# Putting DVE's remainders of one step between the block sums of the next one, in a three-product fp32 matmul

## The reference

```python
w = jnp.einsum('bpf,mf->bpm', features, W_ft) + b_ft      # features (1024, 2, 5128), W_ft (512, 5128), fp32
accumulator = stm * w                                     # stm (1024, 2, 1)
l1_x = jnp.clip(accumulator, 0.0, 1.0).reshape(features.shape[0], -1)
l2_x = jnp.clip(l1_x @ W1.T + b1, 0.0, 1.0)               # W1 (32, 1024)
return l2_x @ W2.T + b2                                   # W2 (1, 32)
```

## Time and profile before

| | us |
|---|---|
| median of 3 runs | 432.38 (429.82 to 434.44) |
| time of the profiled execution | 432.02 |
| its span, first to last instruction | 430.2 |
| PE busy | 407.0 (95%) |
| DVE busy | 349.6 (81%) |
| ACT busy | 196.2 (46%) |
| DMA queue q1, share of 16 engines | 66.9% |
| mean granted TensorE clock | 0.988 of full speed |

### The profile page before, as it was taken

The page is one execution under the profiler, slowest core; times in us unless marked ns, Lnnn a source line. Parts: engine busy times, 40 slices in busy tenths (PEclk is TensorE's granted clock), DMA queues, the critical chain, the costliest instruction groups (busy, mean ns, idle before and its releaser), DMA issues.

```text
span 430.2 us, 4578 instructions
## 1 busy us (share of the span) xinstructions
PE 407.0 (95%) x1756; PEld 323.3 (75%) x1756; DVE 349.6 (81%) x321; ACT 196.2 (46%) x176; POOL 13.2 (3%) x32
## 2 busy tenths in 40 slices
PE   6969999979999989998999999999999899999995
PEld 4747777858777868786878888878788778888862
DVE  3887888896899989979899877897887975698625
ACT  4464454343448444424444674363444448444300
POOL 2090000000000000000000000000000000000000
PEclk9999999989999999998999999999999999999999
DMA  7999797876867666663666766658667766778200
GB/s 237 387 239 269 219 267 247 253 226 200 264 227 244 223 233 235 244 226 143 244 245 244 240 222 237 240 205 337 239 235 238 240 194 195 240 231 254 96 2 0
DMA packets 27300, 96.37 MB, mean 224 GB/s; under 512 B 3432, under 2 KB 6384, under 8 KB 22032
## 3 DMA queue, kind: packets, MB, share of 16 engines
q1 hardware_dynamic: 26656, 95.44, 66.9%
q0 software_dynamic: 624, 0.66, 0.8%
HBM read 96.08 MB, written 0.00 MB: 223 GB/s over the span
## 4 chain that ended last, share of the span: by engine, by line
PE 65%; DMA 15%; DVE 12%; issue 5%; SPq 2%; ACT 1%; DVEq 0%
PE sums L496 63%; DMA xs<-x_p 15%; DVE x_lo L400 5%; DVE w_lo L397 1%; DVE xs L374 1%; PE sums L554 1%; PE sums L598 1%; DVE ws L378 1%; DVE x_lo L352 1%; DVE c_all L413 1%; ACT x_hi L275 0%; SPq L209 0%; DVE c_all L477 0%; DVE ws L364 0%; DVE xr L454 0%
## 5 line engine op out<-in xcount | busy, mean ns | idle before, releaser
L496 PE MATMUL sums<-x_lo,w_hi 128*128 128x512 f32 x560 | 178.0, 396 | 13.8 <-DVE x_lo L400 13.6
L496 PE MATMUL sums<-x_hi,w_hi 128*128 128x512 f32 x560 | 178.0, 396 | 3.2 <-ACT x_hi L264 2.3
L496 PE MATMUL sums<-x_hi,w_lo 128*128 128x512 f32 x560 | 177.2, 395 | 0.2 <-DVE w_lo L347 0.2
L289 ACT ACTIVATE x_hi<-xs 128x2048 fp32r<-128x2048 f32 x67 | 128.7, 1921 | 79.6 <-DVE xs L384 34.9
L400 DVE TENSOR_TENSOR x_lo<-xs,x_hi 128x2048 fp32r<-128x2048 f32 x67 | 153.0, 2284 | 0.0
L496 PEld LDWEIGHTS sums<-x_lo,w_hi 128*128 128x128 f32 x560 | 104.9, 190 | 42.2 <-issue 21.0
L496 PEld LDWEIGHTS sums<-x_hi,w_hi 128*128 128x128 f32 x560 | 106.4, 191 | 29.2 <-ACT x_hi L264 2.8
L496 PEld LDWEIGHTS sums<-x_hi,w_lo 128*128 128x128 f32 x560 | 106.8, 191 | 23.5 <-DVE w_lo L347 0.6
L284 ACT ACTIVATE w_hi<-ws 128x512 fp32r<-128x512 f32 x67 | 42.5, 634 | 116.9 <-PE sums L496 42.1
L397 DVE TENSOR_TENSOR w_lo<-ws,w_hi 128x512 fp32r<-128x512 f32 x67 | 45.9, 684 | 14.7 <-DMA ws<-w_p 14.7
L384 DVE TENSOR_TENSOR xs<-xs 128x2048 f32<-128x2048 f32 x20 | 45.8, 2288 | 8.0 <-DMA xs<-x_p 8.0
(11 more groups left out here) (59 smaller groups left out, 88.7 us busy)
## 6 DMA issues: line engine op xcount, KB each, us to landing
xs<-x_p SPq DMA_DIRECT2D x40, 1024.0 KB, 5.6
xs<-x_p SPq DMA_DIRECT2D x57, 512.0 KB, 5.6
ws<-w_p SPq DMA_DIRECT2D x43, 256.0 KB, 3.2
ws<-w_p SPq DMA_DIRECT2D x17, 384.0 KB, 3.4
ws<-w_p SPq DMA_DIRECT2D x20, 128.0 KB, 4.1
open_x<-x_p SPq DMA_DIRECT2D x2, 512.0 KB, 6.9
stm_all<-stm SPq DMA_DIRECT2D x1, 1024.0 KB, 7.5
open_x<-x_p SPq DMA_DIRECT2D x2, 256.0 KB, 3.8
```

Source lines behind the costliest of these rows:

```text
L289: nc.scalar.activation(x_hi[:, g % HI, :, :], x_pair(g), ACT.Copy).then_inc(x_hi_ready, 1)
L496: return nc.tensor.matmul(sums[:, bank, :], w[:, wslot, wpos, m * P:(m + 1) * P], x[:, xslot, xpos, c * BANK:(c + 1) * BANK], start=start, ...
```

## The change

`sums_of` is split into `w_sums_of` (w sum, in pass 0 also the kept one) and `x_sums_of`, and `low_step` into `w_low` and `x_low`. The loop now calls, for step g: w_low(g), w_sums_of(g+1), x_low(g), x_sums_of(g+1). The small subtraction of g = 8 goes ahead of x_low. In the opening `sums_of` is still one piece, but its kept w sum now stands ahead of its x sum. The instructions are the same ones, in the same number; SP's, ACT's and PE's programs are the same.

```diff
--- before.py
+++ after.py
@@ -353,49 +353,61 @@
                                             x_hi[:, g, pos, a:b].bitcast(F32), ALU.subtract)\
                         .then_inc(open_lo, 1)
 
-            def sums_of(g):
+            def w_sums_of(g):
                 f, k = pass_of(g)
-                i, j, n = raw_w(g, 0), raw_x(g, 0), g % RAW
-                opening = g < OPEN
+                i, n = raw_w(g, 0), g % RAW
                 dve.wait_ge(w_loaded[n], w_count(g))
                 if f == 0:
-                    if opening:
+                    if g < OPEN:
                         dve.wait_ge(open_w_loaded[g], 16)
                     nc.vector.tensor_tensor(ws[:, i + 1, :], ws[:, i + 1, :], ws[:, i + 2, :], ALU.add)\
                         .then_inc(w_sum, 1)
+                    dve.wait_ge(w_sum, g + 1)
+                    a11 = open_w[:, g, :] if g < OPEN else ws[:, i, :]
+                    nc.vector.tensor_tensor(ws[:, KEPT + k, :], ws[:, i + 1, :], a11, ALU.subtract)\
+                        .then_inc(s_kept, 1)
+                elif f == 1:
+                    nc.vector.tensor_tensor(ws[:, i, :], ws[:, i, :], ws[:, i + 1, :], ALU.subtract)\
+                        .then_inc(w_sum, 1)
+                elif f == 2:
+                    dve.wait_ge(s_kept, K_PAIRS)
+                    nc.vector.tensor_tensor(ws[:, i + 1, :], ws[:, i + 1, :], ws[:, KEPT + k, :], ALU.subtract)\
+                        .then_inc(w_sum, 1)
+
+            def x_sums_of(g):
+                f, k = pass_of(g)
+                j, n = raw_x(g, 0), g % RAW
+                if f == 0:
                     dve.wait_ge(t_loaded[n], t_count(k))
-                    if opening:
+                    if g < OPEN:
                         dve.wait_ge(open_x_loaded[g], 16)
                         if g == 0:
                             dve.wait_ge(open_x_loaded[OPEN], 16)
                     else:
                         dve.wait_ge(x_loaded[n], x_count(g))
-                    b11 = open_x[:, g, :] if opening else xs[:, j, :]
+                    b11 = open_x[:, g, :] if g < OPEN else xs[:, j, :]
                     nc.vector.tensor_tensor(xs[:, TST + k, :], xs[:, TST + k, :], b11, ALU.subtract)\
                         .then_inc(x_sum, 1)
-                    dve.wait_ge(w_sum, g + 1)
-                    a11 = open_w[:, g, :] if opening else ws[:, i, :]
-                    nc.vector.tensor_tensor(ws[:, KEPT + k, :], ws[:, i + 1, :], a11, ALU.subtract)\
-                        .then_inc(s_kept, 1)
                 elif f == 1:
-                    nc.vector.tensor_tensor(ws[:, i, :], ws[:, i, :], ws[:, i + 1, :], ALU.subtract)\
-                        .then_inc(w_sum, 1)
                     dve.wait_ge(x_loaded[n], x_count(g))
                     nc.vector.tensor_tensor(x_pair(g), xs[:, j + 1:j + 2, :].broadcast_to([P, 2, COLS]),
                                             x_pair(g), ALU.subtract).then_inc(x_sum, 1)
                 elif f == 2:
-                    dve.wait_ge(s_kept, K_PAIRS)
-                    nc.vector.tensor_tensor(ws[:, i + 1, :], ws[:, i + 1, :], ws[:, KEPT + k, :], ALU.subtract)\
-                        .then_inc(w_sum, 1)
                     dve.wait_ge(x_loaded[n], x_count(g))
                     nc.vector.tensor_tensor(xs[:, j + 1, :], xs[:, j + 1, :], xs[:, TST + k, :], ALU.subtract)\
                         .then_inc(x_sum, 1)
 
-            def low_step(g):
+            def sums_of(g):
+                w_sums_of(g)
+                x_sums_of(g)
+
+            def w_low(g):
                 dve.wait_ge(s_kept, min(g + 1, K_PAIRS))
                 dve.wait_ge(w_hi_ready, later(g))
                 nc.vector.tensor_tensor(w_lo[:, g % RAW, 0:2, :], w_pair(g),
                                         w_hi[:, g % HI, :, :].bitcast(F32), ALU.subtract).then_inc(w_lo_ready, 1)
+
+            def x_low(g):
                 dve.wait_ge(x_hi_ready, later(g))
                 nc.vector.tensor_tensor(x_lo[:, g % RAW, :, :], x_pair(g),
                                         x_hi[:, g % HI, :, :].bitcast(F32), ALU.subtract).then_inc(x_lo_ready, 1)
@@ -441,13 +453,16 @@
             third = 2 * K_PAIRS
             fourth = 3 * K_PAIRS
             for g in range(OPEN, STEPS):
+                w_low(g)
                 if g + 1 < STEPS:
-                    sums_of(g + 1)
+                    w_sums_of(g + 1)
                 if g == 8:
                     dve.wait_ge(rest_loaded, 16 * 8)
                     nc.vector.tensor_tensor(wr_raw[:, 2, :], wr_raw[:, 2, :], wr_raw[:, 0, :], ALU.subtract)\
                         .then_inc(rest_signed, 1)
-                low_step(g)
+                x_low(g)
+                if g + 1 < STEPS:
+                    x_sums_of(g + 1)
                 if g == 12:
                     dve.wait_ge(rest_hi, 2)
                     for q in (32, 96):
```

## The result

The changed kernel takes 440.16 us (median of 4 runs, 439.62 to 441.21); the kernel before, run beside it as well, 431.1 (426.91 to 434.44). The ratio is 1.0246, with a 95% interval of 1.0162 to 1.0331: slower, by 1.6% at least. I had predicted 438.5, with a range of 434 to 446.

A forecast was written before the change was run, and what follows sets the result against it. PE bounds the kernel, with short stops from late loads through DVE's order. Step 19 7.3 us earlier, step 39 6.0 later and step 59 6.4 later gave a span of 436.6; forecast 438.5 us, range 434 to 446.

The forecast's parts named there:

- The closed round: x_lo(g), x_sum(g+1), x_hi(g+1), x_lo(g+1) in series across DVE and ACT: 6.47 us in pass 1, 5.41 in passes 0 and 2.
- The waits for loads: Main loop: x loads get until x_sum(g+1) behind x_lo(g), over 4 us remain, so the stops for loads go.
- The step of g = 12: Pass 0: DVE's remainders of the rest add 2.8 us, of which a lead of some 1.6 absorbs all but 1.2.
- The border of passes 0 and 1: ACT's drain waits behind x_hi(21); PE stands 5.5 us ahead of step 20; x_lo(22) ends at T + 19.1.
- T: End of x_lo(19), the last of pass 0, predicted at 119.1 us; later times are counted from it.
- the border of passes 1 and 2: Same drain delay with the narrow x sum: PE stands 2.5 us; x_lo(42) ends 17.4 us after x_lo(39).
- Pass 2: 17 rounds of 5.41 plus 4.5 us of DVE's other work: x_lo(59) ends at 362.1, step 59 done at 369.5.
- The sum: Whole kernel: step 59 at 369.5 against 363.1, +6.4 us on the 430.2 span, so 436.6; forecast time 438.5.
- A: Rival, faster: pass 1's round closes below 6.1 us; at 5.44 or less about 424 us; 5 in 100.
- B: Rival, within 1%: round right, but T and all behind it move by 2 to 3 us; 435.5; 14 in 100.
- C: Rival, much slower: PE's clock falls in pass 1, up to +10 us in 17 steps, 448; 10 in 100.
- The kept w sum's wait: Opening: the kept w sum, now ahead of the x sum, waits for the instruction before it, costing 0.11 us more.

The follow-up runs named there:

- shorter copy in either order: ACT rounds only half of x in pass 1: in the changed kernel 423.84 us; in the kernel before 430.93 us.
- the halves: Changed kernel with the x sum, x_hi and x_lo of pass 1 each cut in two, same work: 421.92 us.
- the passes apart: Changed kernel with the old order for sums of steps 21 to 39: 423.98 us; the reverse, new order only there: 441.39 us.
- the one with the kept sum last: Changed kernel with the opening's kept w sum put back behind the x sum: 439.06 us.
- the hybrid with early drains: Changed kernel with the old order for sums of steps 21 to 39 and ACT's drains one step earlier: 424.92 us; without the earlier drains 423.98.
- the kernel with the other work spread: Changed kernel with x in halves in pass 1 and drains one step earlier (420.44 us), plus DVE's other work cut into one piece a step: 414.5 us.

## Why the prediction was right

**The closed round** held: 6.48 us measured for 6.47, 5.41 for 5.41. The shorter copy in either order, the halves, and the passes apart all bear it out. **The waits for loads** went: the groups of the three x sums show no idle time in front of them after the change (15.2, 8.0 and 17.5 us before), and 6.9 us were won up to step 19 where I had 7.3. **The step of g = 12** came out near its size by two errors that half cancel. DVE in order of time, from x_lo(12) to x_lo(13), and PE:

```profile
75.87 2.29 DVE L412 TENSOR_TENSOR x_lo<-xs,x_hi 128x2048 fp32r<-128x2048 f32 x1 [0.59 <-ACT x_hi L289]
...
84.48 2.29 DVE L412 TENSOR_TENSOR x_lo<-xs,x_hi 128x2048 fp32r<-128x2048 f32 x1
```

```profile
86.92 0.70 PE L511 MATMUL sums<-x_lo,w_hi 128*128 128x512 f32 x2 [1.18 <-DVE x_lo L412]
87.46 0.62 PE L511 MATMUL sums<-x_hi,w_lo 128*128 128x512 f32 x2
```

The turn is 84.48 - 75.87 = 8.61 us, 3.2 over 5.41 where I had 2.8: the kept w sum fills part of the wait for x_hi, so 0.59 of it is left for other work and not 0.9. PE's lead took 1.8 of that and not 1.6, and step 13 came out 1.44 longer than 5.44, for 1.2. PE's clock did not fall there (granted 1.00 from 86.9 to 92.2).

**The border of passes 0 and 1** had the right stop (5.41 for 5.5) and a wrong step behind it. I took ACT's drain as what x_hi(22) waits for. ACT in order of time, the place of the earlier trace rows:

```profile
129.78 4.00 ACT L301 ACTIVATE c_all<-sums 128x512 f32<-128x512 f32 x8
133.60 0.69 ACT L284 ACTIVATE w_hi<-ws 128x512 fp32r<-128x512 f32 x1
134.44 1.91 ACT L289 ACTIVATE x_hi<-xs 128x2048 fp32r<-128x2048 f32 x1
```

In the kernel before, the x_hi(22) of the earlier trace rows followed its w_hi 0.52 us later:

```profile
134.60 0.69 ACT L284 ACTIVATE w_hi<-ws 128x512 fp32r<-128x512 f32 x1
```

Now it came 0.84 us later, when x_sum(22) ended at 134.40. So the round was never broken: 20 turns of 6.48 from x_lo(19) to x_lo(39), 129.6 us, where I had 129.1. The drain on ACT hid in the 4 us that ACT idles in each turn. My own round says as much: three turns of 6.47 end at T + 19.4, later than the T + 19.1 by way of the drain, and the later of the two had to be taken. That is 0.3 of the 0.5 us; 0.01 a turn is the rest. At the border of passes 1 and 2, with its narrow sum, the drain did lengthen one turn (6.59 us in place of 5.41), and x_lo(42) ended 17.4 us behind x_lo(39), as said.

**Pass 2** came out as said (115.0 for 114.8), but its setter was named wrongly. I had put DVE's path (362.1 for x_lo(59)) ahead of PE's. The list of waits from 258 us on has no wait for x_lo at all: x_lo(59) ended at 362.83 (360.54 + 2.29), and PE, after its stop of 2.35 us and some 2.0 us of slow clock in step 40, came to step 59 at about 363.4 (370.62 less 32 matmuls of 0.227). Each step from 41 to 58 took PE its 5.44 us. The two paths lay within about half a us, so either gave the number, and that part of it is luck: "worth nothing" for the clock at that border was wrong.

**The sum**: +7.6 on the span for +6.4. Of the 1.2 too little, 0.4 lie up to step 19, 0.5 in pass 1 and 0.2 in pass 2. The sum's last step was also written 0.3 short: 438.4 and the 0.4 by which the execution profiled lay below the median make 438.8, not 438.5.

**Rivals.** A did not happen, and the half copy shows where it would have: with a turn of 5.63 the kernel is faster than before. B needed a T earlier by 2 to 3 us; x_lo(19) ended at 119.2, for 119.1. C did not happen in pass 1: the granted clock from 140 to 248 us is 1.00, at stops recorded as 0.77 us in each step. Its price was wrong as well: with a fall in every second step PE needs 7.04 + 5.44 = 12.48 us for two steps, less than two rounds (12.94), so it would have cost nothing. The Trainium skill ("TensorE: Matmul & The Clock Gate", section "HAM oscillation — how this bites in real kernels") describes a loop whose waits, of some 3 to 5 us, bring the clock down in every turn. The waits of every turn here are far shorter, and in this trace, from 24 us on, the clock fell behind the stops of 2.03, 5.41 and 2.35 us alone. **The kept w sum's wait**: 0.11 us for a wait on the instruction in front, as DVE's rows in the opening show (start to start 0.45 in place of 0.34):

```profile
16.01 0.42 DVE L363 TENSOR_TENSOR ws<-ws 128x256 f32<-128x256 f32 x1
16.46 0.43 DVE L367 TENSOR_TENSOR ws<-ws,open_w 128x256 f32<-128x256 f32 x1
16.80 1.22 DVE L389 TENSOR_TENSOR xs<-xs,open_x 128x1024 f32<-128x1024 f32 x1
```

The Trainium skill ("VectorE: DVE Perf Modes", section "The DRAIN you can't avoid") has it, from a row of tensor_copy, that a semaphore after each DVE operation costs nothing extra; for these tensor_tensor rows that does not hold, at a size of a tenth of a us.

## What to carry to other kernels

Before moving work on one engine, follow the loop through all engines: if a step's last product on DVE needs a copy from ACT, and the copy needs a sum that now stands behind the former step's last product, the step can never take less than the three together, however idle both engines are. Keep one step of look-ahead between the two engines, or cut the three in halves so that they overlap; then the order that lets late loads pass is worth having (421.9 us with the same work, against 440.2 for the changed kernel, and 432.1 for the kernel before beside it). A long stop of the bounding engine is worth only what no other path takes back behind it: 7.8 us of stops gave nothing in one kernel and the same edit 1.5 us in another, and six us lay in work that could be cut into pieces fitting an idle gap.

## What the runs showed of the hardware that I had not expected

The same stop does not always bring the clock down. In the changed kernel and in the one with the kept sum last PE stood 2.03 and 2.04 us ahead of the same matmul of step 3. First the changed kernel, then the other, PE in order of time:

```profile
29.45 1.17 PE L511 MATMUL sums<-x_lo,w_hi 128*128 128x512 f32 x2 [2.03 <-DVE x_lo L412]
30.42 1.05 PE L511 MATMUL sums<-x_hi,w_lo 128*128 128x512 f32 x2
```

```profile
28.59 0.70 PE L518 MATMUL sums<-x_lo,w_hi 128*128 128x512 f32 x2 [2.04 <-DVE x_lo L419]
29.13 0.63 PE L518 MATMUL sums<-x_hi,w_lo 128*128 128x512 f32 x2
```

In the first the clock fell to 1.2 GHz (granted 0.50 from 29.5 to 32.9 us) and step 3 was done at 36.4; in the second it stayed at 2.4 GHz (1.00) and step 3 was done at 33.9. It is not the edit that makes the difference. Nine of the traces have a stop of 2.02 to 2.05 us at this matmul, and eight of them have the same opening. From the end of the stop to the end of the step, five of the eight took 6.9 us and three 5.3 (the changed kernel and the hybrid with early drains, and the kernel with the other work spread). So two executions can differ by 1.6 us for this alone.

PE then came earlier to step 13, where DVE was late in both, and stood 2.71 us there in place of 1.18; its clock did not fall (granted 1.00 from 86.3 to 91.6). In the hybrid with the early drains a stop of 2.71 us at the same step was followed by eight pairs in 6.6 us (87.59 to 94.20) in place of 3.6, with the clock at 0.50, so 3.0 us of delay, more than the stop had been; its step 19 was done at 128.4, where the hybrid without had 125.1. First the kernel with the kept sum last, then the hybrid:

```profile
86.31 0.70 PE L518 MATMUL sums<-x_lo,w_hi 128*128 128x512 f32 x2 [2.71 <-DVE x_lo L419]
86.86 0.63 PE L518 MATMUL sums<-x_hi,w_lo 128*128 128x512 f32 x2
```

```profile
87.59 1.19 PE L514 MATMUL sums<-x_lo,w_hi 128*128 128x512 f32 x2 [2.71 <-DVE x_lo L412]
88.58 1.05 PE L514 MATMUL sums<-x_hi,w_lo 128*128 128x512 f32 x2
```

What decides which stops are followed by the slow clock stays open; it was not tried.
